# One piece of a weight maximum moved between reciprocal and context scaling, and a scale moved into the pair scores, in a decoder layer on one core

## What is computed

```python
def bitlinear(x, w):
    xq = _act_quant(_rmsnorm(x))
    wq = _weight_quant(w)
    return jnp.einsum('bsd,ed->bse', xq, wq)
q = bitlinear(x, wq).reshape(B, S, H, Dh)
k = bitlinear(x, wk).reshape(B, S, H, Dh)
v = bitlinear(x, wv).reshape(B, S, H, Dh)
scores = jnp.einsum('bshd,bstd->bsht', q, k) / Dh ** 0.5
attn = jax.nn.softmax(scores, axis=-1)
ctx = jnp.einsum('bsht,bstd->bshd', attn, v)
ctx = jnp.swapaxes(ctx, 1, 2).reshape(B, S, D)
return bitlinear(ctx, wo)
```

## Time and profile before

| | |
|---|---|
| median of 3 runs | 783.32 us (782.77 to 783.34) |
| profiled execution | 779.51 us |
| its span | 777.8 us |
| mean granted TensorE clock | 0.931 |
| TensorE busy | 626.6 us (81%) |
| VectorE busy | 573.6 us (74%) |
| ScalarE busy | 488.9 us (63%) |
| GpSimd busy | 492.7 us (63%) |

### The profile page before, as it was taken

One profiled execution on the slowest core, in us unless ns is written; L12 is line 12 of the kernel. 1 busy time (PEld: TensorE's weight loads), 2 busy tenths in 40 slices (PEclk: granted clock), 3 DMA queues, 4 the chain that ended last, 5 costly groups with the idle time before them and its releaser, 6 DMA issues.

```text
span 777.8 us, 20249 instructions
## 1 busy us (share of the span) xinstructions
PE 626.6 (81%) x6601; PEld 544.6 (70%) x6601; DVE 573.6 (74%) x1717; ACT 488.9 (63%) x994; POOL 492.7 (63%) x669
## 2 busy tenths in 40 slices
PE   2588988888898579999999999897789996778600
PEld 0367877777798468888888888786678885666500
DVE  4998988889874676779778797873585664777464
ACT  4675888778835666777777777564445553355514
POOL 6277777877763744636878777644667764666553
PEclk9699999999999689999999999899799998999955
DMA  6611111121125143443110000100223335221241
GB/s 185 182 18 21 22 22 24 20 24 20 20 36 196 79 165 147 174 168 129 34 37 18 30 24 18 56 24 33 76 73 107 101 98 150 59 74 56 66 112 54
DMA packets 115462, 57.40 MB, mean 74 GB/s; under 512 B 70960, under 2 KB 105968, under 8 KB 115376
## 3 DMA queue, kind: packets, MB, share of 16 engines
q1 hardware_dynamic: 105888, 26.49, 15.2%
q10 hardware_dynamic: 4496, 19.02, 6.3%
q0 software_dynamic: 4992, 10.76, 4.0%
HBM read 22.29 MB, written 33.96 MB: 72 GB/s over the span
## 4 chain that ended last, share of the span: by engine, by line
PE 43%; DVE 28%; issue 12%; ACT 7%; POOL 3%; DMA 3%; SPq 1%; DVEq 1%; ACTq 0%; POOLq 0%
PE PS L1176 12%; PE PS L975 5%; DVE PS L1866 5%; PE PS L1086 4%; PE PS L1096 3%; DVE W_raw L2170 2%; PE PS L1262 2%; PE PS L1279 2%; DVE bn L1822 2%; PE PS L1281 2%; PE PS L1280 2%; PE PS L1264 1%; PE PS L1263 1%; DMA W_raw<-in_L_ffn_W_dram 1%; DVE PS L1870 1%
## 5 line engine op out<-in xcount | busy, mean ns | idle before, releaser
L975 PE MATMUL PS<-prod,ident 128*128 128x144 f32 x1024 | 137.3, 294 | 22.0 <-DVE hctx L1846 21.9
L975 PEld LDWEIGHTS PS<-prod,ident 128*128 128x128 f32 x1024 | 131.5, 195 | 30.8 <-issue 24.9
L750 POOL TENSOR_TENSOR prod<-prod,v 128x2048 f32<-128x2048 f32 x32 | 117.5, 3672 | 33.1 <-ACT prod L1373 33.1
L1176 PE MATMUL PS<-W_raw 128*72 128x128 f32 x1024 | 128.1, 280 | 3.1 <-DVE att L2084 1.9
L870 POOL DMA_INDIRECT ys<-W_raw,ids x92 | 91.2, 991 | 60.1 <-ACT W_raw L1605 28.0
L1176 PEld LDWEIGHTS PS<-W_raw 128*72 128x72 f32 x1024 | 114.5, 146 | 8.5 <-issue 5.1
L2063 DVE TENSOR_REDUCE m<-PS 128x8 f32<-128x1024 f32 x64 | 77.9, 1218 | 43.9 <-PE PS L1096 43.9
L2170 DVE SCALAR_TENSOR_TENSOR W_raw<-PS,W_raw 128x512 f16<-128x512 f32 x92 | 60.7, 688 | 51.8 <-ACT W_raw L1595 51.8
L810 POOL DMA_INDIRECT xs<-Y,spot_u x64 | 63.6, 994 | 24.3 <-issue 14.2
L1866 DVE TENSOR_REDUCE PS<-pair_sq 128x128 f32<-128x1024 f32 x64 | 75.1, 1219 | 0.3
L1281 PE MATMUL PS<-W_lo,W_raw 128*128 x368 | 71.6, 223 | 0.0
(11 more groups left out here) (298 smaller groups left out, 1569.0 us busy)
## 6 DMA issues: line engine op xcount, KB each, us to landing
xs<-pad ACTq DMA_DIRECT2D x16, 1152.0 KB, 4.6
Y<-xs SPq DMA_DIRECT2D x46, 144.0 KB
W_raw<-ys SPq DMA_DIRECT2D x16, 256.0 KB, 5.0
W_raw<-in_L_ffn_W_dram SPq DMA_DIRECT2D x1, 2048.0 KB
shuffle<-hctx SPq DMA_DIRECT2D x32, 64.0 KB, 3.0
Y<-shuffle SPq DMA_DIRECT2D x32, 64.0 KB, 1.8
cs<-in_ctx_dram SPq DMA_DIRECT2D x8, 256.0 KB, 2.9
out_dram<-W_raw SPq DMA_DIRECT2D x8, 256.0 KB, 2.3
```

The source lines that it names most:

```text
L750: pool.tensor_tensor(rows[:, :, 0:D].rearrange("p t (d h) -> p t d h", d=HD), a.broadcast_to((P, H, HD, H)), v.broadcast_to((P, H, HD, H)) ...
L975: last = pe.matmul(PS[:, 6, 0:TC], ident[:], prod2[:, i % 2, TC * t:TC * (t + 1)], start=(t == 0), stop=(t == H - 1))
L1176: last = pe.matmul(PS[0:HO, 7, a * P:(a + 1) * P], v_frame[:, i % 2, a, HO * n:HO * (n + 1)], PT[:, i % 2, 8 * a + n, :], start=(n == 0), ...
```

## The change

It does two things on VectorE, both in the loop. The piece of the maximum is taken between the reciprocal and the scaling of `context` instead of at the slot's end, and the wait for the reciprocal counts only up to the reciprocal (`inverted`), so it does not wait for the piece. And `y_scale` is called inside `pair_scores` of slot 1, behind its three sums, instead of ahead of it. This second part also holds for every slot 1 with there(2), all of which lie in the loop; the calls of `y_scale` behind the loop stay.

```diff
-            def settle(self):
-                self.eng.wait_ge(self.s, self.n + self.turn)
+            def settle(self, n=None):
+                self.eng.wait_ge(self.s, (self.n if n is None else n) + self.turn)
...
-            def context(u, j):
+            def context(u, j, meanwhile=None):
...
                 step(dve.reciprocal(E1inv[:], PS[:, 6, D:TC]))
-                settle()
+                inverted = ch.n
+                if meanwhile:
+                    meanwhile(k)
+                settle(inverted)
                 after_dma(dve, shuffled, k - 5)
...
-            def pair_scores(u, j):
+            def pair_scores(u, j, scale_y=False):
...
+                if scale_y:
+                    y_scale(u - 2)
                 settle()
...
+            def largest_part(k):
+
+                step(dve.tensor_reduce(w2_top[:, bass.ds(k - 2 * TB, 1)], w2_flat[:, bass.ds(W2_STEP * k - 2 * TB * W2_STEP, W2_PART)],
+                                       AX.X, ALU.max, apply_absolute_value=True))
...
                 if there(-((j - 4) // TB)):
-                    context(u, j)
-                if j == 1 and there(2):
-                    y_scale(u - 2)
+                    context(u, j, None if isinstance(u, int) else largest_part)
                 if there(-((j - 1) // TB)):
-                    pair_scores(u, j)
+                    pair_scores(u, j, j == 1 and there(2))
...
-                if not isinstance(u, int):
-                    step(dve.tensor_reduce(w2_top[:, bass.ds(k - 2 * TB, 1)], w2_flat[:, bass.ds(W2_STEP * k - 2 * TB * W2_STEP, W2_PART)],
-                                           AX.X, ALU.max, apply_absolute_value=True))
```

## The result

The changed kernel takes 774.32 us (median of 4 runs, 772.6 to 775.74), the kernel before 783.05 (4 runs, 779.7 to 783.34). The difference of the medians is 8.7 us. The ratio of the runs is 0.9906, with a 95% interval of 0.9883 to 0.9929, and that is 7.4 us less (5.6 to 9.2). The forecast was 7.7. Run again beside its parts the changed kernel took 772.44 against 778.17, 5.7 less by the medians, ratio 0.9901 (0.987 to 0.9932). The medians of the kernel before lie between 778.2 and 783.1 in the three comparisons of this study, so I read the change mostly from the loop, whose length repeats.

What follows compares the result with a forecast made beforehand. VectorE was taken to lead the loop, with TensorE near full. Rounds of 23.13 instead of 24.59 us gave 7.3 over five, 8.6 with laps; 7.7 was taken off 783.32, giving 775.6, range 772.8 to 780.0.

Steps and rivals of the forecast that it cites:

- r(1): Start of the reciprocal in slot 1 of a loop round, the zero from which the forecast counts the round.
- r(2): Start of slot 2's reciprocal: TensorE's sums set it at 5.19 us, VectorE's own work only 5.0.
- r(3): Start of slot 3's reciprocal: TensorE decides at 12.54 us, VectorE would be there at 12.12.
- r(0): Start of the next round's slot 0 reciprocal: 17.8 us against 19.00 before, 1.2 gained.
- The chain through `s2`: From `s2` over `round_y`, `turn_y` and projection to `sum_keys` of slot 2: not before 8.35 us, 0.37 of slack gone.
- the first rival: Chain behind `s2` shorter than thought, VectorE with TensorE's 5.19 us sets a 22.64 round: 10.2 us less, 773.1; chance 0.11.
- Round 2: The loop's first round, ahead of rounds 3 to 7: little to gain, its slot 3 reciprocal just where it was.
- The gap that stays: Rival: register work still follows the piece, scaling 0.24 us later in every slot; 3.5 us less, 779.8; chance 0.14.
- The clock: Rival: TensorE idles 1.6 us in slot 1 and its clock falls; 2.5 us slower, 785.8; chance 0.06.
- lost behind the loop: Part of the rival that nothing comes of it, by this or a thin side path: 783 within 1.5; chance 0.09.
- The side paths: ScalarE's and GpSimd's other work in the loop: costed at nothing, with cover of 0.6 and 0.8 us.
- the prediction's second bound: `sum_keys` of slot 3 held by TensorE's order behind `turn_x`: 13.71 us, beside 13.54 by `hctx`; 13.6 taken.

Runs made afterwards that it cites:

- the longer chain: Changed kernel plus one unread 128-element ScalarE copy ahead of `round_y`: loop 140.31 us against 139.13. Same copy in the kernel before: 147.32 against 147.34.
- small sum first: Changed kernel with slot 1's small third sum taken first and `y_scale` ahead of the last large sum: 771.84 us, against 772.44 for the changed kernel.

## Why the prediction was right

The forecast was 7.7 us less, and the loop gave 8.21. The whole times agree with both, but at 7.4 us with an interval of 5.6 to 9.2 they could not tell the forecast from a good part of its rivals' range; the steps can. Behind r(1) at 170.06:

| step | predicted | measured |
|---|---|---|
| scaling behind the reciprocal | 0.50 | 0.51; 0.57 to 0.61 where the reciprocal had waited |
| `s2` | 3.43 | 3.41 |
| `turn_y` | 6.76 | 6.74 |
| `sum_keys`, slot 2 | 8.35, with the lap 8.20 | 8.17 |
| r(2) | 5.19 | 5.20 |
| r(3) | 12.54 | 12.35 |
| `sum_keys`, slot 3 | 13.6 | 13.43 |
| r(0) | 17.8 | 17.63 |
| r(0) to r(1) | 5.33 | 5.36 and 5.40 |
| round | 23.13 | 23.03 and 22.80 |

**The chain through `s2`** was the main point and stands: the scale freed VectorE of 1.27 us of waiting and came itself 1.1 us late, the slack was used up, and the projection behind `turn_y`, in TensorE's order, took the lead over `hctx` in slot 2. It was shown by the longer chain, which costs its full 0.20 a round here and nothing before. The two kinds of round say the same without an edit: a chain 0.14 longer costs 0.13 in the changed kernel and nothing before. The slack was larger than the 0.37 of idle that the row shows: `s2` came 1.08 later and `sum_keys` of slot 2 only 0.55 later, so it was 0.53. Most of the difference is the lap of the projection: its modelled end runs 0.17 past the start of `sum_keys` in the changed kernel.

**The terms that were off in size.** The end of the chain: I had taken the modelled ends of matmuls at their word and corrected for it only in part, and 7.7 lay between 7.3 without laps and 8.6 with them. The value with the lap was right within 0.03 for `sum_keys` of slot 2. Rounds 3 to 7 gained 8.29 us and round 2 lost 0.08, so the forecast fell 0.5 short in the loop. The sum had also multiplied one kind of round by five, the one with the longer chain. And "TensorE decides" r(3), with VectorE 0.4 us ahead of it, was too clear. VectorE's row at 182.41 has no idle bracket, its last record before that ends at 182.39. Its own work was about 12.25 and not 12.12 (r(3) with the small sum first), since the scaling comes 0.59 and not 0.50 behind a reciprocal that has waited. My reading is that the address rows of the piece and the register work behind its wait are then no longer issued ahead; no run separates them. So the first rival was nearer than its price said: with the chain out of the way the round was 22.70 to 22.83, and not 22.64. TensorE's sums came only 0.02 to 0.10 us behind VectorE's own work, and that the forecast named the right one at r(3) is in part luck.

**The piece.** 0.26 per slot where VectorE leads was 0.19 and 0.23 alone, 2.37 us in the loop. In the changed kernel, where the chain holds slot 2 to 3, it adds 0.87 to what the scale gives alone (140.00 to 139.13). That shows in the loop only: by the whole times, 772.44 with the piece and 772.18 without, nothing can be told. Of the 8.21 us most is the scale's.

**Round 2** was to gain little: 24.58 before (67.82 to 92.40), 24.66 after (6.94, 5.30, 7.14 and 5.28), a loss of 0.08. Right, near enough.

**The rivals.** The gap that stays is out by the scaling at 0.51, though behind a reciprocal that has waited up to 0.1 us of it does stay. The rule of the Trainium skill that a wait on a semaphore costs nothing extra ("VectorE: DVE Perf Modes", "The DRAIN you can't avoid") agrees with the rows behind the loop; in the loop, the 0.25 of idle that comes back when the pieces are taken out disagrees with it as a rule for this place, and what differs is register work between the wait and the scaling. The clock did not fall: 1.43 or 1.58 us of idle before `turn_y` in each round left it at 1.00. The gain was not lost behind the loop, as said above. The side paths held. On ScalarE the cover was less than claimed: `xq` ended at 182.76, where it was forecast, and `turn_x` started sooner, at 183.18, so it was 0.42 instead of 0.6. On GpSimd the product of slot 3 ended at 187.93 and `sum_keys` of slot 0 started at 188.67, 0.74 where 0.8 was claimed.

**Slot 3 to 0** rose to 5.26 to 5.28 from 5.18 to 5.19, and here the prediction's second bound did not decide. It had `sum_keys` of slot 3 held by `turn_x` in TensorE's order, at 13.71, as well as by `hctx`, at 13.54. `turn_x` came 13.12 behind r(1), and without the pieces, with `turn_x` at 13.11, `sum_keys` started at 13.35. In the changed kernel it started at 13.43, 0.49 behind the scaling at 12.94. So the scaling held it, and the scaling was 0.59 behind the reciprocal because the reciprocal had waited for TensorE. Where the reciprocal of slot 3 does not wait (small sum first) the scaling comes 0.48 behind it, and the slot takes 5.16 to 5.18 with the piece in the same place. Without the piece it takes 5.19 to 5.20 though the chain leads. It takes both, the piece and a chain that holds back the reciprocal.

## What to carry to other kernels

In this loop, with wait values in registers, a small operation that nobody waits for cost least between a result and its reader, provided that the wait counts only up to the result. Before a step is moved to where its input is surely there, follow its output through every engine and each engine's own order, and compare with the idle time before the place where it comes back; that row's idle time is the slack, or, behind matmuls with modelled ends, its lower bound (0.37 read, 0.53 found). Beyond the slack each tenth counted in full here. To tell which of two chains leads, lengthen one by a known amount in both kernels.

## What was not expected of the hardware

The same program with the same 2.52 us of idle before a `sum_keys` ran its 32 matmuls once in 5.83 and once in 4.16 us. In the slow one the granted clock was 0.53 in the first 2 us, so at its lower level of 1.2 GHz for nearly all of them, 0.62 in the next 2, and 1.00 behind that; in the fast one it was 1.00 throughout. Over the ten profiles, six had 2.18 to 2.35 us of idle at this place and all six took 4.16. Four had 2.52 to 2.53, and took 5.83, 5.83, 7.12 and 4.16. At the first `sum_keys` of the loop the idle time was 2.44 to 2.56, and nine of ten took 5.86, one 4.19, the one that had taken 7.12 just before. After 1.43 to 1.83 us of idle, once a round, it never was slow. So with about 2.5 us of idle the clock fell in some executions and not in others. The spread of the kernel before (776.2 to 783.8 us over the later comparisons) is larger than the 3.54 us that the transfer and the slow `sum_keys` made between two profiles; how much of it they explain, I did not try to divide.
